# Last pair of heads: softmax denominators turned into 16 columns by small matmuls, inverted there, and spread back by matmuls

## The reference, cut to what matters

```python
probs = jax.nn.softmax(attn, axis=-1)
out = jnp.einsum('bhqk,bhkd->bhqd', probs, v)
out = out.transpose(0, 2, 1, 3).reshape(B, S, D)
return out @ out_w.T + out_b
```

## Time and profile before

| | us |
|---|---|
| median of 3 runs (lowest, highest) | 781.52 (779.87, 783.82) |
| the profiled execution, its own time | 779.61 |
| its span, first to last instruction | 777.8 |
| TensorE matmul busy | 712.5 (92%) |
| VectorE busy | 550.7 (71%) |
| ScalarE busy | 435.9 (56%) |
| GpSimd busy | 288.7 (37%) |

### The profile page before, as it was taken

One profiled execution on the slowest core, in us unless ns is written; L12 is line 12 of the kernel. 1 busy time (PEld: TensorE's weight loads), 2 busy tenths in 40 slices (PEclk: granted clock), 3 DMA queues, 4 the chain that ended last, 5 costly groups with the idle time before them and its releaser, 6 DMA issues.

```text
span 777.8 us, 10975 instructions
## 1 busy us (share of the span) xinstructions
PE 712.5 (92%) x4190; PEld 446.3 (57%) x4190; DVE 550.7 (71%) x896; ACT 435.9 (56%) x579; POOL 288.7 (37%) x273
## 2 busy tenths in 40 slices
PE   3778898969697979999999999999999999999997
PEld 3657787957456868867767676333333433333444
DVE  4897766675557674667888878888888378888416
ACT  2542223345244444243243333999999899999883
POOL 0156865332314566343344343012224213422510
PEclk9898999998799989999999999999999999999999
DMA  6145101000301345334311002344344345342221
GB/s 247 55 155 186 52 0 55 1 1 1 108 0 40 125 155 196 103 106 146 110 55 55 24 32 72 108 131 132 113 138 140 90 133 172 126 131 84 95 85 55
DMA packets 25704, 74.14 MB, mean 95 GB/s; under 512 B 4604, under 2 KB 5980, under 8 KB 24692
## 3 DMA queue, kind: packets, MB, share of 16 engines
q1 hardware_dynamic: 21124, 65.37, 25.1%
q0 software_dynamic: 3808, 7.60, 3.3%
q10 hardware_dynamic: 720, 0.48, 0.2%
HBM read 54.54 MB, written 23.06 MB: 100 GB/s over the span
## 4 chain that ended last, share of the span: by engine, by line
PE 73%; DVE 13%; ACT 5%; issue 4%; POOL 3%; DMA 1%; SPq 0%; DVEq 0%; ACTq 0%; POOLq 0%
PE PS L734 23%; PE PS L996 16%; PE PS L982 11%; PE PS L740 10%; PE PS L965 6%; PE PS L955 4%; DMA stg<-in_wa 1%; DVE mx L1275 1%; DVE XD L1081 1%; PE PS L814 1%; DVE sg L1213 1%; DVE sg L1204 1%; DVE XL L1088 1%; ACT sg L1415 1%; DVE bst L1066 1%
## 5 line engine op out<-in xcount | busy, mean ns | idle before, releaser
L1461 ACT ACTIVATE P<-PS 128x1024 f32<-128x1024 f32 x256 | 249.0, 1024 | 29.9 <-PE PS L982 29.7
L1282 DVE TENSOR_REDUCE mx<-PS 128x1 f32<-128x512 f32 x300 | 189.1, 682 | 32.1 <-PE PS L965 30.5
L1275 DVE TENSOR_REDUCE mx<-PS 128x2 f32<-128x1024 f32 x106 | 124.8, 1220 | 37.9 <-PE PS L955 37.6
L996 PE MATMUL PS<-P,VV 128*32 128x512 f32 x1024 | 136.5, 605 | 0.1
L1538 POOL TENSOR_TENSOR hl<-sg,hh 128x512 fp32r<-128x512 f32 x64 | 83.1, 1299 | 137.1 <-ACT hh L1423 79.9
L982 PEld LDWEIGHTS PS<-QS,KS 64*128 64x128 f32 x512 | 48.4, 183 | 123.2 <-ACT P L1461 110.2
L982 PE MATMUL PS<-QS,KS 64*128 64x512 f32 x512 | 116.6, 456 | 2.3 <-DVE mx L1275 1.8
L965 PE MATMUL PS<-KM,QM 64*128 64x512 f32 x300 | 81.3, 396 | 0.0
L1417 ACT ACTIVATE sg<-PS,cols 128x512 f32<-128x512 f32 x32 | 22.0, 688 | 83.0 <-PE PS L734 83.0
L734 PE MATMUL PS<-XH,UGH 128*128 128x512 f32 x128 | 54.9, 429 | 5.8 <-ACT us L1426 4.9
L1547 POOL TENSOR_TENSOR sg<-sg,us 128x512 f32<-128x512 f32 x32 | 42.1, 1315 | 37.2 <-ACT us L1426 37.2
(11 more groups left out here) (201 smaller groups left out, 1417.5 us busy)
## 6 DMA issues: line engine op xcount, KB each, us to landing
QM<-scr_q SPq DMA_DIRECT2D x16, 512.0 KB, 4.3
KM<-scr_k SPq DMA_DIRECT2D x16, 512.0 KB, 5.3
QS<-scr_q SPq DMA_DIRECT2D x16, 512.0 KB, 4.3
KS<-scr_k SPq DMA_DIRECT2D x16, 512.0 KB, 5.3
scr_q<-spl SPq DMA_DIRECT2D x24, 256.0 KB, 3.3
scr_k<-spl SPq DMA_DIRECT2D x24, 256.0 KB, 3.6
scr_o<-OE POOLq DMA_DIRECT2D x14, 256.0 KB, 2.7
stg<-in_tern SPq DMA_DIRECT2D x3, 1024.0 KB, 4.8
```

Source lines behind the costliest of these rows:

```text
L996: i = e.matmul(PS[32 * c:32 * c + 32, 7, :], v_head(8 * b + kt, 2 * j + c // 2), P[s % 4][:, chunk(c // 2 + 2 * (c % 2))], start=(kt == 0) ...
L1275: e.tensor_reduce(mx[p % 2][:, :, qt, half], PS[:, b:b + 2, :], AX.X, ALU.max).then_inc(q["mx"], 2)
L1282: e.tensor_reduce(mx[p % 2][:, h, qt, half:half + 1], bank[b], AX.X, ALU.max).then_inc(q["mx"], 1)
L1461: e.activation(P[s % 4][:, half * 1024:(half + 1) * 1024], PS[:, b:b + 2, :].rearrange("p b n -> p (b n)"), ACT.Exp).then_inc(q["ex"], 1)
```

## The change

On TensorE, `last` now starts with 6 of the 24 matmuls of pairs 12 to 14. Then it makes four matmuls with OE[1] as the stationary operand (128 columns of queries) and four columns of SEL as the moving one: the 4 x 512 denominators come out as 128 x 16. VectorE takes the reciprocal of these 16 columns into RL, and copies them into RB, each column repeated 32 times (128x512). Four matmuls of RB against the identity turn that into a 128x512 tile of reciprocals in two PSUM banks, and VectorE multiplies OE[1] by it, straight from PSUM. The two reciprocals of 128x256 are gone. On VectorE both multiplications now stand ahead of both subtractions. One more PSUM bank is used (seven in all), the banks are dealt in another order, RB and RL take SBUF at 156 KB and 158 KB, and there is one semaphore more (`lb`). ScalarE's and SyncE's code is unchanged.

```diff
-                put("last", list(range(6)))
+                put("last", [1, 2, 3, 4, 5, 6, 0])
...
+        RB = sb("RB", 156, [128, 512])
+        RL = sb("RL", 158, [128, 16])
...
             def last(banks):
                 halves = [slice(0, 256), slice(256, 512)]
-                den, acc = banks[:2], banks[2:]
-                e.wait_ge(d["wl"], 32)
-                for i, qs in enumerate(halves):
-                    claim(den[i])
-                    e.wait_ge(q["lo"], i + 1)
-                    e.matmul(bank[den[i]][:, 0:256], SEL[:, :], OE[1][:, qs], start=True, stop=True).then_inc(q["lden"], 1)
-                e.wait_ge(q["gl"], 4)
-                for n, b in enumerate(acc):
-                    claim(b)
+                den, *wide_den = banks[:3]
+                acc = banks[3:]
+
+                def others(n):
+
+                    claim(acc[n])
                     for r in range(2):
                         ts = slice((2 * n + r) * 128, (2 * n + r + 1) * 128)
-                        two_tiles(bank[b], r, ((OH[1][:, ts], WOH[:, 1, :]), (OH[1][:, ts], WOL[:, 1, :]), (OL[1][:, ts], WOH[:, 1, :])), True, False)
+                        two_tiles(bank[acc[n]], r, ((OH[1][:, ts], WOH[:, 1, :]), (OH[1][:, ts], WOL[:, 1, :]), (OL[1][:, ts], WOH[:, 1, :])), True, False)
+
+                e.wait_ge(q["gl"], 4)
+                others(0)
+                claim(den)
+                e.wait_ge(d["wl"], 32)
+                for t in range(4):
+                    if t % 2 == 0:
+                        e.wait_ge(q["lo"], t // 2 + 1)
+                    o = e.matmul(bank[den][:, 4 * t:4 * t + 4], OE[1][:, t * 128:(t + 1) * 128], SEL[:, 0:128:32], start=True, stop=True)
+                o.then_inc(q["lden"], 1)
+                others(1)
+                for b in wide_den:
+                    claim(b)
+                e.wait_ge(q["lr"], 2)
+                for t in range(4):
+                    ts = slice(t * 128, (t + 1) * 128)
+                    o = e.matmul(bank[wide_den[t // 2]][:, ts], RB[:, ts], IDN[:, :], start=True, stop=True)
+                    if t % 2 == 1:
+                        o.then_inc(q["lb"], 1)
+                others(2)
+                others(3)
                 e.wait_ge(q["wl"], 2)
...
             def last(banks):
                 halves = [slice(0, 256), slice(256, 512)]
+                den, *wide_den = banks[:3]
+                acc = banks[3:]
+                e.wait_ge(q["lden"], 1)
+                e.reciprocal(RL[:, :], bank[den][:, 0:16]).then_inc(q["lr"], 1)
+                e.wait_ge(q["lr"], 1)
+                e.tensor_copy(RB[:, :].rearrange("p (c o) -> p c o", o=32), RL[:, :].rearrange("p (c o) -> p c o", o=1).broadcast_to([128, 16, 32])).then_inc(q["lr"], 1)
+                e.wait_ge(d["late0"], 16)
                 for i, qs in enumerate(halves):
-                    e.wait_ge(q["lden"], i + 1)
-                    if i == 0:
-                        e.wait_ge(d["late0"], 16)
-                    e.reciprocal(OE[0][:, qs], bank[banks[i]][:, 0:256]).then_inc(q["lr"], 1)
-                    e.wait_ge(q["lr"], i + 1)
-                    e.tensor_tensor(OE[0][:, qs], OE[1][:, qs], OE[0][:, qs], ALU.mult).then_inc(q["ln"], 1)
+                    e.wait_ge(q["lb"], i + 1)
+                    e.tensor_tensor(OE[0][:, qs], bank[wide_den[i]][:, qs], OE[1][:, qs], ALU.mult).then_inc(q["ln"], 1)
+                for i, qs in enumerate(halves):
                     e.wait_ge(q["lh"], i + 1)
                     e.tensor_tensor(LL[:, qs], OE[0][:, qs], r32(LH[:, qs]), ALU.subtract).then_inc(q["ll"], 1)
```

More of the change, by code:

```diff
@@ L38 @@
 mt mx mc mr ma sc ex pv oe rcp gm gh gl pj pjx wl fill
-lo lden lr ln lh ll lp ly
+lo lden lr lb ln lh ll lp ly
 """.split()
@@ L1330, in last @@
                         e.wait_ge(q["lp"], 2 * i + cc + 1)
-                        e.tensor_tensor(xs, bank[banks[2 + 2 * cc + i]], xs, ALU.add).then_inc(q["ly"], 1)
+                        e.tensor_tensor(xs, bank[acc[2 * cc + i]], xs, ALU.add).then_inc(q["ly"], 1)
             parts = {f.__name__: f for f in (start, ln_stats, ln_norm, ln_turn, bias, w0l, signs, tern_scale, tern_cut, add_vb, half, scales, kv_in, kv_sums, q0,
```

## The result

The changed kernel takes 778.75 us, the median of 16 runs (777.61 to 779.77); the kernel before takes 780.55 us in its 16 runs beside them. One of these 16 took 2221.61 us and counts in that median, but not in the comparison. The ratio is 0.9971, 95% interval 0.9960 to 0.9981: 2.3 us less, between 1.5 and 3.1. Without the one long run the means lie 2.3 us apart (780.93 and 778.64), the medians only 1.5 (780.24 and 778.75). The prediction had 1.0 us less. The time lies in its range and the direction is right, but the interval of the difference lies wholly above what was forecast. The profiled execution took 777.61 us, with a span of 775.8.

What follows compares the result with a forecast made beforehand. VectorE was taken to bound the end before the change, TensorE after it. The last addition's end moving from 775.15 to 774.12 us gave 1.0 less, so 781.52 became 780.5 us, range 778.3 to 782.4.

Steps and rivals of the forecast that it cites:

- 1: first narrow product starts: TensorE first issues six products of pairs 12 to 14, 0.72 us plus 0.1, hiding ScalarE's copies.
- 7: last addition ends: VectorE's additions to X follow every six products; only the last, 0.68 us, lies behind TensorE, ending at 774.12.
- Step 2: Four narrow products on TensorE, OE as weights and 4 moving columns: 8 records of 0.11 us, 0.88 in all.
- Step 3: VectorE inverts 16 columns in 0.25 us and copies them to 512 in 0.43, or 0.68 at the slower rate.
- Step 4: Four spreading products of 128 columns on TensorE: 8 records of 0.11 us, 0.9 in all.
- Step 6: TensorE's last 12 products of pairs 12 to 14, then pair 15's 24, make it the last in, to 773.28.
- A: The forecast itself: 1.0 us less, time 780.5 on the scale of the median; chance 0.77.
- B: Gain eaten: narrow products' loads not hidden (0.72 more), copy takes 0.68 (0.25 more); time 781.5, chance 0.12.
- D: More than forecast: narrow records cost 0.07 and switches between kinds are hidden; gain 1.6, time 779.9, chance 0.08.
- C: Slower: TensorE's clock falls at about 767 if it is nearly idle; 3.1 us slower, time 784.6, chance 0.03.
- the output's DMAs, which the change leaves alone: After the last addition the span runs on 2.65 us with the output's DMAs, taken as unchanged.
- 781.52 - 1.0: Step from the end's gain to the time: the median before less 1.0 us, giving 780.5.

Runs made afterwards that it cites:

- wide_copy: The kernel before with both wide reciprocals replaced by copies of the same shape, leaving out the last pair's division; tail 8.12 us.
- low_between: The changed kernel with VectorE's subtraction put back between the two multiplications; tail 8.77 us.
- placebo: The kernel before with the change's extra semaphore and two SBUF tiles declared but not used; ratio 0.9995, the second time 1.0003.
- again2: The changed kernel unaltered, measured a third time against the kernel before; ratio 0.9986, tail 8.75 us.
- turn_both: The changed kernel with its eight small float32 products made transposes; ratios to the kernel before 0.9966 and 0.9964, tail 8.08 us.

## Why the prediction was right and where it failed

The tail, by the steps of the prediction, each time counted from the end of the last `values` (765.25 in the forecast, 764.57 in the trace):

| step | forecast | measured |
|---|---|---|
| 1: first narrow product starts | 0.72 | 0.74 |
| 2: reciprocal of 16 columns starts | 1.75 | 1.73 |
| 3: RB is written | 2.50 | 2.45 |
| 4: spread starts | 2.63 | 2.60 |
| 6: first product of pair 15 starts | 5.15 | 5.00 |
| 7: last addition starts | 8.19 | 8.08 |
| 7: last addition ends | 8.87 | 8.77 |

- Step 2: a narrow record took 0.10 (765.31 to 766.12 for 8), forecast 0.11. The bounds of 0.07 and 0.20 were far, and the row was the right one to stand near.
- Step 3: the copy took 0.43, the rate of the cast in the earlier trace rows. A source that repeats each element 32 times from SBUF does not slow it. The Trainium skill's rule of two results per cycle ("VectorE: DVE Perf Modes", section "Mode 2×_2P") holds for it as well.
- Step 4: a spreading record took 0.11 (767.17 to 768.05 for 8), as in the earlier trace rows. The 81 ns of the Trainium skill ("TensorE: Matmul & The Clock Gate", section "Back-to-back issue gap") do not fit a float32 record of 128 columns here.
- Step 6, that TensorE takes over as the bound, came true, but its first term was too large: 0.18 for the switch from the spread to the next product, where the trace has 0.08 (768.05 to 768.25, less the usual 0.12). The tail came out 0.10 shorter than forecast. That TensorE bounds was tried four ways: less work on it shortens the tail, a wrong order or no cover lengthens it by what is put off, and moving VectorE's work about changes nothing.
- Rivals: A's mechanism is what the trace shows, 1.13 off the tail against 1.03. B did not happen, since loads flow at 0.10 and the copy is fast. D named a larger gain, but neither of its causes is there: a narrow record took 0.10, not 0.07, and each switch to these products still cost about 0.1 (764.49 to 764.71, less 0.12). C, the clock, did not happen; it stayed at 1.00. Its condition, an idle as long as the 4.16 us of the earlier trace rows, was too strict: in wide_copy the clock was 1.00 from 486 to 490 us, with TensorE busy for 2.08 of the 4 us and no wait above 1.18, and 0.66 from 490 to 495. low_between has nearly the same waits there (1.19 the longest) and kept 1.00. The windows of wide_copy:

```profile
486.00:490.00 4.00, 2.08 (x11) 1.08 (x12) 4.00 (x6) 2.40 (x3) 0.48 (x1) 1.00 0.34 86
490.00:495.00 5.00, 4.95 (x26) 1.92 (x28) 3.28 (x6) 3.19 (x4) 1.40 (x2) 0.66 0.00 0
```

- Two sentences of the working are loose. The 24 products of pairs 12 to 14 end at about 769.8, so the first reciprocal (to 768.28) hides only part of them, and the multiplication, rounding and subtraction behind it the rest. And the small products are 16 records in place of 4, not 16 more. Neither changes the sum.

What failed is the size, in two places. The smaller is a term that was put at nothing without a reason: "the output's DMAs, which the change leaves alone". They took 0.19 us less behind the last addition. Before, the four additions came 0.62 apart; now TensorE spaces them 0.72 apart, and I infer that the last store started when the one before had gone further. All kernels with additions 0.7 apart have an output of 2.45 to 2.56 us, all with 0.62 have 2.64 to 2.70. wide_copy belongs to the first kind: its code is that of before but for the reciprocals, its additions are 0.72 apart, and its output is 2.49. So the spacing goes with the gain even where none of the changed code is there; what the stores do inside was not looked at.

The larger is the step from the sum to the time, "781.52 - 1.0". It took "everything before about 765 us" as "the same work", so that the times would differ by the tail alone. The work is the same, but the time it took in the traces was between 764.57 and 769.29, and went with the granted clock. That failed twice. The base of 781.52, a median of three, lay 1.3 above the median of the 15 runs in the comparison, so the forecast of 780.5 was above even the median of before (780.24), and that 778.75 lies in the range is owed to the width that was given to scatter. And the difference was measured as 2.3 where the trace has 1.3: in the comparison 3 of the 15 runs of before took 782.7 or more and none of the changed kernel's 16, which moves the means more than the medians (1.5 apart). The two repeats came to 1.9 and 1.1, and the placebo speaks against anything that the declarations move. The pooled medians are still 1.9 apart, where tail and output give 1.3. Whether that 0.6, and with it the lack of long executions in the changed kernel, is chance or something that the traces do not show stays open. The prediction also named a sign of being wrong, that the stretch before 765 "moves by more than 1 us". It could not serve: it moved by 1.45 in again2, and by 2.21 in the placebo, which changes nothing. The chance of 0.96 for a difference within 0.5% was right.

## What to carry to other kernels

Price a change at the end of a program on every engine that is there, not only on the one that bounds now: here 3.45 us were removed from VectorE, 1.8 was the most that could come out in the old order of TensorE, and the small matmuls that made it possible took part of that back. If an operation costs by the element, like a reciprocal, invert the distinct values alone, and look for the cheapest way to turn and spread them: a transpose left one record where a float32 product against the identity left two. Fill waits with work that needs nothing, ahead of the thing that waits, and compare stretches between two fixed points of the trace where whole executions scatter by more than the change. Look at the spread of the times as well as at their ratio: a few long executions on one side moved a mean here by more than half of what the change was worth.

## What the runs showed of the hardware

- A reciprocal on VectorE costs by the element: 0.25 us for 16 columns and 1.75 for 256, 6.3 ns a column in between. From a PSUM bank 16 columns took 0.26, and with a step of 32 columns 0.26 as well.
- Eight float32 weight loads of 128 columns with only 4 moving columns flow at 0.10 us a record; the same with 128 moving columns at 0.11. So 4 moving columns cost nearly as much as 128.
- A float32 transpose of 128x128 left one record and followed its neighbour by 0.09 (turn_both, four from 766.67 to 767.02), with the granted clock at 1.00.
- Of one and the same program, the clock granted in the first 20 us was 1.00 or 0.70 to 0.72, and the times of its executions spread over 4 to 5 us. The two do not go together one to one: over all traces with 1.00 the last `values` ended between 764.57 and 769.29. The mean clock from 40 to 80 us sorts these ends better (0.91: up to 765.92; 0.87: 766.70 to 768.54; 0.83: 768.23 and 769.29).
- One fall of the clock at 490 to 495 us, 0.66 instead of 1.00, went with a last `values` 1.06 us later (wide_copy against low_between, whose clocks in the windows up to 120 us agree).
